# A four-layer graph GRU on one core: VectorE's sum moved to the head of the next step, TensorE's passes onto r times hn moved ahead of the transposes

## What is computed

```
for l in range(4):
    m = x @ weight[l]
    agg = segment_sum(m[src], dst, num_segments=n_nodes)
    gi = agg @ w_ih.T + b_ih          # split into i_r, i_z, i_n
    gh = x @ w_hh.T + b_hh            # split into h_r, h_z, h_n
    r = sigmoid(i_r + h_r)
    z = sigmoid(i_z + h_z)
    n = tanh(i_n + r * h_n)
    x = (1 - z) * n + z * x
out = layernorm(node_embed + (x + node_embed))
```

## Time and profile before

| | |
|---|---|
| median of 3 runs | 2386.39 us (2386.11 to 2389.7) |
| profiled execution | 2389.03 us, span 2387.2 us |
| granted TensorE clock | 0.988 of full, on average |
| PE busy | 94% of the span |
| DVE busy | 86% |
| ACT busy | 77% |
| POOL busy | 71% |

### The profile page before, as it was taken

One profiled execution on the slowest core, in us unless ns is written; L12 is line 12 of the kernel. 1 busy time (PEld: TensorE's weight loads), 2 busy tenths in 40 slices (PEclk: granted clock), 3 DMA queues, 4 the chain that ended last, 5 costly groups with the idle time before them and its releaser, 6 DMA issues.

```text
span 2387.2 us, 48608 instructions
## 1 busy us (share of the span) xinstructions
PE 2239.4 (94%) x11728; PEld 1906.8 (80%) x11728; DVE 2053.6 (86%) x3927; ACT 1833.7 (77%) x3483; POOL 1689.6 (71%) x1654
## 2 busy tenths in 40 slices
PE   3999999999899999999999999999988888988886
PEld 2888888888788888888788888888777777777774
DVE  7788888888688888888688888888779999998987
ACT  1688888888678888888678888888747777777776
POOL 3887777777487777777487777777477777777773
PEclk7999999999999999999999999999999999999998
DMA  2455555555456666666556666656534555554553
GB/s 56 123 160 160 161 160 159 162 157 161 121 162 171 171 171 168 172 172 167 146 146 172 171 167 172 172 167 169 168 100 135 145 142 144 141 145 141 147 142 109
DMA packets 277062, 362.43 MB, mean 152 GB/s; under 512 B 107754, under 2 KB 186586, under 8 KB 276980
## 3 DMA queue, kind: packets, MB, share of 16 engines
q1 hardware_dynamic: 238118, 309.12, 44.0%
q0 software_dynamic: 38784, 52.30, 9.7%
q10 hardware_dynamic: 78, 0.08, 0.0%
HBM read 208.71 MB, written 179.20 MB: 162 GB/s over the span
## 4 chain that ended last, share of the span: by engine, by line
PE 55%; DVE 21%; ACT 12%; issue 8%; DMA 1%; DVEq 1%; POOL 1%; ACTq 0%; POOLq 0%; SPq 0%
PE pZ L852 15%; PE pR L852 7%; PE pHN L852 7%; PE pA L840 7%; DVE diff L1457 4%; PE pO L939 4%; DVE diff L1451 4%; PE pA L852 4%; PE pIN L852 4%; DVE aggT L1414 3%; ACT o_rows L1132 3%; ACT a_hi L1083 3%; PE pR L893 2%; PE pR L896 2%; PE pR L894 2%
## 5 line engine op out<-in xcount | busy, mean ns | idle before, releaser
L688 POOL DMA_INDIRECT gath<-state,idx x900 | 932.7, 1036 | 267.0 <-issue 251.7
L665 POOL TENSOR_TENSOR h_lo<-hT,h_hi 128x250 fp32r<-128x250 f32 (+2 forms) x400 | 345.9, 865 | 286.2 <-DVE diff L1457 282.9
L1083 ACT CAST a_hi<-aggT 128x500 fp32r<-128x500 f32 x396 | 241.9, 611 | 330.8 <-DVE aggT L1414 330.8
L688 POOL DMA_INDIRECT gath<-in_x_dram,idx x300 | 320.4, 1068 | 101.8 <-issue 71.1
L1457 DVE TENSOR_TENSOR diff<-pZ,diff 128x500 f32<-128x500 f32 x400 | 271.4, 678 | 40.7 <-issue 0.5
L1096 ACT ACTIVATE rg<-pR,bsum 128x500 f32<-128x500 f32 x400 | 270.3, 676 | 44.2 <-PE pR L896 26.8
L1405 DVE TENSOR_TENSOR a_lo<-aggT,a_hi 128x500 fp32r<-128x500 f32 x396 | 269.1, 680 | 5.4 <-ACT a_hi L1083 4.7
L1078 ACT CAST sel<-sel 128x504 fp32r (+1 forms) x400 | 244.2, 611 | 31.7 <-DVE flag_i L1388 29.6
L1414 DVE TENSOR_TENSOR aggT<-pA,hT 128x500 f32<-128x500 f32 x396 | 264.9, 669 | 3.3 <-PE pA L840 3.3
L1108 ACT ACTIVATE pZ<-pZ,bsum 128x500 f32<-128x500 f32 x400 | 257.4, 643 | 9.4 <-PE pZ L852 9.4
L852 PE MATMUL pZ<-a_hi,wf_hi 128*128 128x500 f32 x400 | 190.7, 477 | 66.2 <-DVE diff L1457 66.0
(11 more groups left out here) (215 smaller groups left out, 6323.1 us busy)
## 6 DMA issues: line engine op xcount, KB each, us to landing
columns<-newT SPq DMA_DIRECT2D x300, 250.0 KB, 2.7
hT<-columns SPq DMA_DIRECT2D x300, 250.0 KB, 2.7
state<-o_rows SPq DMA_DIRECT2D x300, 224.0 KB
x_rows<-in_x_dram SPq DMA_DIRECT2D x200, 224.0 KB
out_dram<-o_rows SPq DMA_DIRECT2D x91, 224.0 KB
gath<-state,idx POOLq DMA_INDIRECT x900, 2.5
state<-o_rows SPq DMA_DIRECT2D x297, 26.0 KB
idx<-edge_src SPq DMA_DIRECT2D x395, 1.5 KB
```

What stands on the lines that cost most here:

```text
L665: nc.gpsimd.tensor_tensor(part_of(h_lo, u)[:, cols], hT[:, u % RING, cols], part_of(h_hi, u)[:, cols].bitcast(F32), ALU.subtract).then_inc ...
L688: pool.indirect_dma_start(out=gath[:, u % RING, j, :], out_offset=None, in_=states[l], in_offset=bass.IndirectOffsetOnAxis(ap=idx[:, u % R ...
L1083: nc.scalar.copy(by_rows(a_hi[:, u % RING, :]), sums_of if summed else by_rows(aggT[:, :])).then_inc(s_ahi, 1)
```

## The change

Three things move, no operation is added or left out.

VectorE: the sum of block b+1 stands at the head of step b, ahead of the difference of b-1, where the sum of b+2 stood in the middle of it; a_lo of b+1 stands at the end of the step, where a_lo of b+2 stood. ScalarE: a_hi of b+1 stands behind tanh of b-1, no longer ahead of z's gate. In layer 0 the row copy stays ahead of r's gate and the two copies of the state of b+3 stand behind it; in the other layers it is the other way round. In the last layer the four scaled copies stand together between r's gate and z's. TensorE: the passes of n onto r times hn stand behind z, ahead of the transposes of the new state and of x.

```diff
--- before.py
+++ after.py
@@ -971,7 +971,7 @@
-                        if last:
+                        if onto:
                             n_onto_r_times_hn(l, b, u)
@@ -980,8 +980,6 @@
-                        if onto and not last:
-                            n_onto_r_times_hn(l, b, u)
@@ -1179,18 +1175,18 @@
                         if not ramp:
+                            if exists(i, u, 1):
+                                high_part(l, *after(i, u, 1)[:2])
+                            if l:
+                                high()
+                            else:
+                                rows(i, u)
+                        r_gate(l, b, u, first and l == 0)
+                        if ramp and u == 3:
+                            high_part(l, 4, 4)
+                        if ramp or l:
                             rows(i, u)
-                            high()
-                        fresh = half_done(i, u, OUTLAG) if final else None
-                        if not fresh:
-                            normal(i, u, 0)
-                        r_gate(l, b, u, first and l == 0)
-                        if fresh:
-                            normal(i, u, 0)
-                        if ramp:
-                            if u == 3:
-                                high_part(l, 4, 4)
-                            rows(i, u)
+                        if ramp or l == 0:
                             high()
@@ -1202,18 +1198,14 @@
+                        normal(i, u)
                         if not seeded(i, u):
                             n_gate(u, l * ADDED_APART + b + 1)
                         if ramp and u < 3:
                             high_part(l, *after(i, u, 1)[:2])
-                        if not ramp and exists(i, u, 2):
-                            high_part(l, *after(i, u, 2)[:2])
                         z_gate(l, b, u)
-                        normal(i, u, 1)
                         if ramp and u != 1:
                             widen(l, {0: 2, 2: 5, 3: 6}[u], {0: 2, 2: 5, 3: 6}[u])
-                        if ramp and u == 3:
-                            high_part(l, 5, 5)
@@ -1541,6 +1532,8 @@
+                        if not ramp and exists(i, u, 1):
+                            aggregate(l, *after(i, u, 1)[:2])
                         if exists_before(i, u, ADDED_APART + 1):
                             difference(l, *after(i, u, -1)[:2])
                             product(l, *after(i, u, -1)[:2])
@@ -1557,8 +1550,8 @@
-                        summed = after(i, u, 1 if ramp else 2)[:2] if exists(i, u, 2) else None
-                        if summed and not (ramp and u == 3):
+                        summed = after(i, u, 1)[:2] if exists(i, u, 1) and not (ramp and u == 3) else None
+                        if ramp and summed:
                             aggregate(l, *summed)
@@ -1577,18 +1570,14 @@
-                        if summed and not (ramp and u == 3):
+                        if summed:
                             low_part(l, *summed)
-                        if ramp and u == 3:
-                            aggregate(l, 5, 5)
...
-                        if ramp and u == 3:
-                            low_part(l, 5, 5)
```

More of the change, by code:

```diff
@@ L1124, in last_rows_out, with normalise @@
                               o_rows[PARTS[1], u, :]).then_inc(s_store[u], 16)
[L1126 to L1131, removed]
+            def normalise(u, stored, shifted):
+                act.wait_ge(s_store[u % RING], 32 * stored)
+                act.wait_ge(s_nmr, shifted)
+                for k in range(RPP):
                     last = nc.scalar.activation(o_rows[:, u % RING, k * D:(k + 1) * D], y_rows[:, u, k * D:(k + 1) * D],
                                                 ACT.Identity, bias=nmr[:, u, k:k + 1], scale=rstd[:, u, k:k + 1])
-                if part:
-                    last.then_inc(s_o, 1)
+                last.then_inc(s_o, 1)
             def normalise_in_place(u, shifted, columns):
@@ L1156, in rows, with normal @@
                             rows_out(l, pb, pu, earlier(turn(pi, pu)))
-                    def normal(i, u, part):
+                    def normal(i, u):
                         if final and exists_before(i, u, lag):
                             pb, pu, pi = after(i, u, -lag)
-                            normalise(pu, earlier(turn(pi, pu)), turn(pi, pu) + 1, part)
+                            normalise(pu, earlier(turn(pi, pu)), turn(pi, pu) + 1)
                     def step(i, u, first, last):
@@ L1242, in one @@
                         else:
-                            for part in range(2):
-                                normalise(0, l * NB + b, b + 1, part)
+                            normalise(0, l * NB + b, b + 1)
                     one_by_one(act, one)
```

## The result

The changed kernel takes **2406.92 us** (median of 4 runs, 2403.1 to 2407.39) against 2387.89 us (2386.11 to 2389.7) for the kernel before, measured beside it: 1.0076 times as long, 95% interval 1.006 to 1.0092. The forecast was 2414.

What follows compares the result with a forecast made beforehand. Bound: TensorE's chain in layers 0 to 2, a ring through VectorE, ScalarE and TensorE in layer 3. 57 - 14 - 14 - 2 = +27 on 2389.03 gives 2416; less 2.6 to the median, 2414 us; range 2389 to 2438.

Steps and rivals of the forecast that it cites:

- ScalarE's order in layer 0: Layer 0: h_hi behind r's gate makes GpSimd's h_lo meet VectorE's operations; +0.65 us x 88 blocks = +57 us.
- The stop: Layer 0, each block: VectorE stands still 1.1 us when sel or g_lo meets GpSimd's h_lo; range 0.9 to 1.3.
- The wait behind a_lo: VectorE: the sum directly behind a_lo waits for it, 0.15 us a block, range 0 to 0.19; TensorE covers layers 1, 2.
- The rival that it is free: VectorE's sum waits for a_lo at no cost, layer 0's stop stays: 2387 us, no change; chance 0.07.
- Layers 1 and 2: Both layers then run at TensorE's pace: -0.08 us x 88 blocks x 2 = -14 us.
- that rival: Layers 1 and 2: a late gather pushes h_lo into g_lo, 44 us more, without the 14 won: 2470 us; chance 0.05.
- Layer 3: Of 0.42 us a block to be had, 0.15 goes for the wait, 0.11 for meetings: 0.16 x 90 = -14 us.
- a meeting: Layer 3: VectorE meets GpSimd, late behind the square root, once in five blocks, 0.55 us each, 0.11 a block.
- the 2 us for the first steps of a layer: First steps of a layer: one sum and one a_lo fewer, made at the end beside TensorE; -2 us over all.
- TensorE's half: TensorE's passes onto r times hn before the transposes: tanh can start 0.44 us earlier, by itself worth nothing.
- The rival that the stop costs nothing: Layer 0 stays at TensorE's 5.65 us a block: 2356 us, 2346 without layer 3's meetings; chance 0.12, at about 2352.

Runs made afterwards that it cites:

- the two runs: Changed kernel with TensorE's old order: 2403.31 us; kernel before with TensorE's new order alone: 2388.58 us.
- the last kernel above: Changed kernel with state copies ahead of r's gate in layer 0, two buffers for aggT, all 500 h_lo columns on GpSimd in layer 3: 2337.91 us.

## Why the prediction was right

The sign and the place were right, the time 7 us too high; the sum was 27, the two medians differ by 19.

- *ScalarE's order in layer 0* was predicted at +57 and measured +52.4. h_lo was to start 3.47 and sel 3.39 behind the sum; both came at 3.42. The stop is 0.99 where 1.1 was taken. The detail that failed is who is stopped. I had sel lose, because in the opening a sel that began 0.18 ahead had lost. Here sel held, GpSimd waited for it (1.61 instead of 1.07), and g_lo lost, in 86 of 86 blocks. That is what the rule of the Trainium skill (SBUF — State Buffer, "SBUF: two separate sides") gives, whoever starts first holding the lock for the whole instruction; the trace agrees here, and not in the opening. The loss was nearly the same either way, so this error cost the forecast little. VectorE's work of 5.05 is 5.04 by its own terms (3.67, 0.59 and 0.78).
- *The wait behind a_lo* was taken at 0.15 and measured 0.17 in layer 0 and 0.15 in layer 3, there in four of five blocks. The rival that it is free falls: without the wait the kernel is 27 us faster. The sentence "the semaphore costs nothing extra here" of the Trainium skill (VectorE: DVE Perf Modes, "The DRAIN you can't avoid") was measured there on a row of eight tensor copies; it doesn't carry over to this wait on the instruction just ahead.
- *Layers 1 and 2*: -14 predicted, -15 measured. z is back at 1.40. They don't meet, so that rival falls too.
- *Layer 3*: -14 predicted, -19.7 measured with the end of the kernel. Two terms were too large: a meeting costs 0.45 in the mean (VectorE's short h_lo is stopped, late in GpSimd's), not 0.55, and the wait counts in four blocks of five, 0.12 a block and not 0.15. Between the sum of 27 and the spans' 17.5 lie 9.5 us: 4.6 of them in layer 0, 5.7 here, 1 in layers 1 and 2; against them stand the 2 us for the first steps of a layer, which no run shows apart.
- *TensorE's half* at nothing: right within the noise of the two runs, and in layer 1 for the reason given: tanh stands behind a_hi and z's gate.
- *The rival that the stop costs nothing* was priced at about 2352. With the stop taken away the kernel takes 2356, so its price stands; its condition didn't.
- What I got wrong later, in the expectation for the late copies in the kernel before, is the same meeting there. I carried a stop of 1.0 over to a case in which h_lo starts 0.2 to 0.6 before sel and stops it for 0.61, about what VectorE had to spare.

## What to carry to other kernels

When an edit moves an instruction on one engine, follow what its result releases on the others, and put that start beside what the other engines run at that moment, measured from one common event: two copies put behind the row copy and r's gate on ScalarE made GpSimd's h_lo start 3.42 us behind VectorE's sum, where it starts 2.4 behind it with the copies first. So it met VectorE's operations with two SBUF operands, and that cost 51 us where all else in the change gained 32. A stop counts only for what the engine has no idle time to absorb, so a meeting that is free before a change can cost in full after it. A second buffer takes away a wait on the instruction just ahead, which cost 0.15 to 0.17 us each time here.

## What the runs showed of the hardware that was not expected

- GpSimd is stopped too. Its h_lo takes 1.61 when sel starts level with it, and the mean goes from 1186 to 1676 ns; in the meetings of the opening it had kept its 1.08 to 1.27.
- Within some 0.25 us the profiled start doesn't say who holds. sel at 119.90 began 0.18 ahead of GpSimd and was stopped. In the 86 blocks of layer 0 of the changed kernel sel began between 0.12 ahead and 0.01 behind, and was never stopped. In layer 3 of the last kernel above a_lo began 0.09 to 0.26 ahead and was stopped in 17 of 17 meetings, to 2.00 at 2020.69. What decides between them stays open.
- A stopped operation of VectorE ended 0.41 after GpSimd's in g_lo's case, 0.54 in sel's (303.09 against 302.55 in the kernel before with late copies) and in a_lo's (2022.69 against 2022.15); VectorE's h_lo of 150 columns in layer 3 ended 0.17 after it (2021.98 against 2021.81). From start to start such operations take 0.47, 0.59 and 0.22 when nothing stops them, so nearly all of the work is done after GpSimd's.
- One and the same wait behind a_lo makes the sum start 0.70, 0.86 or 0.97 after it, depending on the block. In the long case the chain shows two steps of VectorE's sequencer and 0.24 of issue between them; why only some blocks have them is open.
